# Flamingo-style gated block (cross attention and mixture of experts) on one core: merged constant loads, x by partition, and another order of the first steps

## What is computed

```python
ln_out = _ln(hidden_states, ln_w, ln_b)          # a layernorm of a layernorm
q  = _ln(_fp8_linear(ln_out, wq,  wq_scale,  q_in_scale))    # 16 heads of 128
k  = _ln(_fp8_linear(ln_out, wk,  wk_scale,  k_in_scale))    # 8 heads
v  =     _fp8_linear(ln_out, wv,  wv_scale,  v_in_scale)
qx = _ln(_fp8_linear(ln_out, wqx, wqx_scale, qx_in_scale))
kx, vx = split(ctx @ w_kv_x.T); kx = _ln(kx)
out = _fp8_linear(concat(attend(q, k, v), attend(qx, kx, vx)) / smooth, wproj, ...)
# _fp8_linear(x, w, ws, s) = (round_to_fp8(clip(x / s)) * s) @ w.T * ws
```

## Time and profile before

| | |
|---|---|
| median of 3 runs | 438.38 us (436.29 to 438.97) |
| profiled execution | 438.61 us |
| its span, first to last instruction | 436.8 us |
| mean granted TensorE clock | 0.969 |
| PE busy | 387.8 us (89%) |
| VectorE (DVE) busy | 352.9 us (81%) |
| ScalarE (ACT) busy | 294.6 us (67%) |
| GpSimd (POOL) busy | 278.0 us (64%) |

### The profile page before, as it was taken

The page is one execution under the profiler, slowest core; times in us unless marked ns, Lnnn a source line. Parts: engine busy times, 40 slices in busy tenths (PEclk is TensorE's granted clock), DMA queues, the critical chain, the costliest instruction groups (busy, mean ns, idle before and its releaser), DMA issues.

```text
span 436.8 us, 11224 instructions
## 1 busy us (share of the span) xinstructions
PE 387.8 (89%) x3626; PEld 288.6 (66%) x3626; DVE 352.9 (81%) x804; ACT 294.6 (67%) x621; POOL 278.0 (64%) x379
## 2 busy tenths in 40 slices
PE   0577799999999999999999999999998497999970
PEld 0445567667667767676766777676687286999960
DVE  5867979999999998999999999999889762334336
ACT  2598788777877777876877787787973315666510
POOL 2068866886787687688588677765574750366650
PEclk9999999999999999999999999999989688999995
DMA  8960868999980000000000000000194213444308
GB/s 209 261 228 2 106 90 259 253 287 286 243 230 3 0 0 0 0 0 0 0 0 0 0 0 0 0 2 2 33 434 194 96 67 98 124 132 136 99 22 277
DMA packets 34621, 45.57 MB, mean 104 GB/s; under 512 B 2970, under 2 KB 32031, under 8 KB 33696
## 3 DMA queue, kind: packets, MB, share of 16 engines
q1 hardware_dynamic: 26368, 35.34, 27.4%
q0 software_dynamic: 6944, 9.46, 9.9%
q10 hardware_dynamic: 1280, 0.41, 0.5%
HBM read 28.21 MB, written 24.19 MB: 120 GB/s over the span
## 4 chain that ended last, share of the span: by engine, by line
PE 73%; DVE 11%; ACT 4%; DMA 4%; issue 3%; POOL 3%; POOLq 0%; ACTq 0%; SPq 0%; DVEq 0%
PE proj_ps L972 18%; PE proj_ps L964 8%; PE score_ps L1001 8%; PE pv_ps L1024 8%; PE headT_ps L990 6%; PE out_ps L1034 6%; PE proj_ps L1138 4%; PE headT_ps L1138 3%; PE score_ps L990 3%; PE probT_ps L1010 3%; DMA cenf<-in_cen 2%; PE score_ps L1153 1%; DVE xs L1702 1%; DVE arena L1326 1%; PE pv_ps L1153 1%
## 5 line engine op out<-in xcount | busy, mean ns | idle before, releaser
L972 PE MATMUL proj_ps<-arena 128*128 128x512 f16 x384 | 100.0, 383 | 3.0 <-DVE arena L1356 3.0
L1364 DVE BATCH_NORM_STATS2 st<-rot 128x6 f32<-128x256 f32 x192 | 72.6, 419 | 10.6 <-ACT rot L710 10.0
L572 POOL TENSOR_TENSOR rot<-rot,cw 128x512 f32<-128x512 f32 x64 | 77.9, 1238 | 2.5
L710 ACT ACTIVATE rot<-proj_ps 128x512 f32<-128x512 f32 x96 | 56.1, 585 | 7.6 <-PE proj_ps L972 6.0
L972 PEld LDWEIGHTS proj_ps<-arena 128*128 (+1 forms) x384 | 32.5, 98 | 32.3 <-issue 3.8
L642 POOL DMA_INDIRECT ybuf<-arena,bslot x31 | 30.5, 984 | 31.3 <-DVE bslot L1612 14.6
L731 ACT ACTIVATE rot<-rot,cw 128x128 f32<-128x128 f32 x128 | 40.9, 391 | 11.0 <-POOL cw L566 10.4
L578 POOL TENSOR_TENSOR reg<-reg,rinv 128x512 f32<-128x512 f32 x32 | 33.4, 1044 | 21.9 <-DVE rinv L1374 21.9
L964 PE MATMUL proj_ps<-arena 128*128 128x512 f16 x192 | 46.7, 379 | 0.6 <-POOL arena L528 0.6
L1024 PEld LDWEIGHTS pv_ps<-reg,vv 64*128 64x128 f32 x512 | 31.1, 187 | 12.9 <-issue 9.7
L990 PE MATMUL headT_ps<-idf,rot 128*128 128x128 f32 x256 | 38.5, 273 | 0.1
(11 more groups left out here) (229 smaller groups left out, 850.2 us busy)
## 6 DMA issues: line engine op xcount, KB each, us to landing
zbuf<-fill SPq DMA_DIRECT2D x1, 16576.5 KB, 65.5
arena<-in_wffn SPq DMA_DIRECT2D x4, 1536.0 KB, 13.4
arena<-zbuf SPq DMA_DIRECT2D x30, 128.5 KB, 2.2
wkv_stage<-in_wkvN SPq DMA_DIRECT2D x1, 2048.0 KB, 15.4
wp_sb<-in_wpT POOLq DMA_DIRECT2D x1, 2048.0 KB, 16.4
wp_sb<-ybuf SPq DMA_DIRECT2D x8, 256.0 KB, 4.5
xs<-in_x SPq DMA_DIRECT2D x2, 512.0 KB, 5.5
vv<-in_wqN POOLq DMA_DIRECT2D x1, 1024.0 KB, 12.5
```

What stands on the lines that cost most here:

```text
L572: gp.tensor_tensor(r, r, cw[:, 4 * i:4 * i + 4].unsqueeze(2).to_broadcast([P, 4, D]), ALU.mult)\
L710: act.activation(raw[c % 2][i], proj_ps[i % 2][:, :], ACT.Copy).then_inc(proj_evac, 1)
L972: mm = pe.matmul(ps, lhs, w[kind][:, ch, 512 * b:512 * b + 512], start=(k == 0), stop=(k == 3))
L1364: ins = ve.bn_stats(st[:, 4 * i + h:4 * i + h + 2, :].rearrange("p h s -> p (h s)"), raw[c % 2][i][:, h * D:(h + 2) * D].rearrange("p (h d ...
```

## The change

The constants `colv`, `idf` and `cenf` become one array of 316 columns and one load; `rowv`, `trif` and `slots` become another of 186 columns. x is laid out by partition in HBM and loaded in three pieces: tile 0, tiles 1 to 3, tiles 4 to 7. VectorE takes the statistics of tile 0 first, has its root taken alone, and takes those of the other tiles around it; the other tiles are scaled by a second Newton step after tile 0's grid, and all of them are normalised there. PE transposes tile 0 before folds 0 and 1, then has both halves of the other transposes and folds 2 to 5 before step 0; ScalarE's list is changed to match.

```diff
+XG = [(0, 1), (1, NT // 2), (NT // 2, NT)]
+NCONST = NCOL + 2 * P
+NTABLE = NROWV + P + NT * TOPK
+EARLY = 6
@@ tiles
-        colv = sb("colv", [P, NCOL], F32)
...
+        consts = sb("consts", [P, NCONST], F32)
+        colv, idf, cenf = consts[:, 0:NCOL], consts[:, NCOL:NCOL + P], consts[:, NCOL + P:NCONST]
+        tables = sb("tables", [P, NTABLE], F32)
...
-            return range(4, NFOLD) if isinstance(n, int) and n == 0 else range(0)
+            return range(EARLY, NFOLD) if isinstance(n, int) and n == 0 else range(0)
@@ SP
-            for half in range(2):
-                sp.dma_start(xs[:, half * NHT * H:(half + 1) * NHT * H].rearrange("p (t d) -> p t d", t=NHT),
-                             x[half * NHT * P:(half + 1) * NHT * P, :].rearrange("(t p) d -> p t d", p=P))\
-                  .then_inc(ld_x[half], 16)
+            for i, (t0, t1) in enumerate(XG):
+                sp.dma_start(xs[:, t0 * H:t1 * H], x[:, t0 * H:t1 * H]).then_inc(ld_x[i], 16)
@@ ScalarE
-            act.dma_start(colv[:, :], cols).then_inc(ld_cols, 16)
-            act.dma_start(idf[:, :], ident).then_inc(ld_small, 16)
-            act.dma_start(cenf[:, :], cen).then_inc(ld_small, 16)
-            act.dma_start(rowv[:, :], rowc).then_inc(ld_route, 16)
-            act.dma_start(trif[:, :], tri).then_inc(ld_route, 16)
-            act.dma_start(slots[:, :], slot).then_inc(ld_route, 16)
+            act.dma_start(consts[:, :], cols).then_inc(ld_cols, 16)
+            act.preload_act_table(ACT.Tanh)
+            act.dma_start(tables[:, :], rowc).then_inc(ld_route, 16)
...
-            act.wait_ge(ld_small, 32)
...
-            root(0, tw[:, 0, :], tw[:, 1, :], tw[:, 2, :])
+            root(0, tw[:, 0, 0:1], tw[:, 1, 0:1], tw[:, 2, 0:1])
...
-            for j in range(2):
-                fold_high(j)
             act.wait_ge(xT0_done, 1)
             for c in range(HC):
                 act.activation(xT[:, c, 0:P], proj_ps[1][:, c * P:(c + 1) * P], ACT.Identity,
                                scale=col("lnw", c), bias=col("lnb", c)).then_inc(xT0_evac, 1)
+            for j in range(2):
+                fold_high(j)
+            root(1, tw[:, 0, 1:NT], tw[:, 1, 1:NT], tw[:, 2, 1:NT])
...
             inputs_out(0)
-            for j in range(2, 4):
+            inputs_out(1)
+            for j in range(2, EARLY):
                 fold_high(j)
...
-                if isinstance(n, int) and n == 0:
-                    inputs_out(1)
@@ PE
-            pe.wait_ge(ld_small, 32)
-            pe.wait_ge(cen_done, 1)
-            for j in range(2):
-                fold(j)
+            pe.wait_ge(ld_cols, 16)
             pe.wait_ge(xn_done, 1)
             for c in range(HC):
                 mm = pe.transpose(proj_ps[1][:, c * P:(c + 1) * P], xn[:, c * P:c * P + P], idf[:, :])
             mm.then_inc(xT0_done, 1)
+            pe.wait_ge(cen_done, 1)
+            for j in range(2):
+                fold(j)
...
             input_transposes(0)
+            input_transposes(1)
...
-                if isinstance(n, int) and n == 0:
-                    input_transposes(1)
...
-            for j in range(2, 4):
+            for j in range(2, EARLY):
                 fold(j)
@@ VectorE
+            row_stats(0, 1, ld_x[0])
+            inputs_variance(0, 1)
             ve.memset(oneh[:, :], 1.0)
             ve.memset(fill[:, 0:H], 0.0)
...
+            row_stats(1, NHT, ld_x[1])
+            inputs_scale(0, 0, 1)
...
             rows_normal(0, 1)
-            rows_normal(1, NHT)
+            row_stats(NHT, NT, ld_x[2])
+            inputs_variance(1, NT)
+            ve.wait_ge(tanh_done, 1)
+            ve.tensor_scalar(gate[:, 0:1], th[:, 0:1], col("s_proj"), None, ALU.mult)
+            link(ve.tensor_copy(gate[:, 1:2], th[:, 1:2]))
+            link(ve.tensor_scalar(gate[:, 2:3], gate[:, 0:1], col("s_pin"), None, ALU.mult))
...
-            for j in range(2):
-                fold_low(j)
-
...
                              .to_broadcast([P, 4, HC, P]), ALU.mult).then_inc(xin_done, 1)
+            for j in range(2):
+                fold_low(j)
             inputs_clip(0)
...
             ve.tensor_tensor(xq[:, 0:XW], ys[:, :], xm[:, :], ALU.subtract).then_inc(xgrid_done, 1)
+            inputs_scale(1, 1, NT)
+            rows_normal(1, NHT)
             rows_normal(NHT, NT)
-            for j in range(2, 4):
+            for j in range(2, EARLY):
                 fold_low(j)
```

52 lines of the change are left out of this document (23 added, 29 removed).

## The result

The changed kernel took 445.94 us (median of four runs, 443.42 to 446.70), the kernel before 437.71 us beside it (436.29 to 438.97): ratio 1.0179, interval 1.0126 to 1.0232. It is slower, by 8.2 us where 3.1 were forecast. The profiled execution took 446.70 us with a span of 444.9, that is 8.1 us over the span of before. The two ratios stand for 7.8 and 5.8 us, and their intervals together reach from 3.6 to 10.2.

The account below looks back on a forecast made before the run. The start's chain through VectorE, ScalarE and GpSimd was taken as the bound. First projection 6.2 us later, 3.0 given back by ScalarE, Ln 3.1 later: 438.61+3.1 = 441.7, less 0.23, so 441.5 us; range 438.0 to 446.0.

Parts of the forecast that it names:

- L, the constants: Start, ScalarE's queue: the merged constants land at 4.7 us, between 4.2 and 7.1, letting VectorE begin.
- Rival C: Start, ScalarE's queue: merged constants take two turns, landing at 7.1; VectorE's list moves 2.4 us, total 443.9; chance 0.12.
- Grid of tile 0: VectorE's list up to the first projection: 13.2 us from the constants, grid ready at 17.9, 1.5 us before the old 19.4.
- Grid to first projection: Second Newton, tiles 1 to 3, transposes and folds 2 to 5 hold the first projection to 25.7, 6.2 us later.
- First projection to its evacuation: PE's first projection: its result comes 1.9 us after its start, at 27.6, with 0.5 less as the other end.
- Evacuation to Ln: ScalarE's list: fold 6 follows after 0.5 us, then 8.44 us as before; Ln at 36.5, 3.1 us later.
- Ln to step 1's variance: GpSimd's unchanged list carries the Ln's shift to step 1's variance, about 13.3 us behind the Ln.
- rival B: x's last load waits behind wq, landing near 13; VectorE stands about 3 us, total 444.5; chance 0.17.
- phase of the later loop and measurement 1 us: Allowance of 1 us among this case's own unknowns, in the range 440 to 443.5.
- A: Tile 0's gain carries: first projection at the grid, before 22.5, with 3.0 us of ScalarE's list gone; 433.9 us; chance 0.06.
- D: Absorbed: a wait behind step 2 hides the late start, or the start is not bound as read; 438.4 us; chance 0.12.

Follow-up runs that it names:

- merged_only: Kernel before with only the merged constant and table loads and the Tanh table loaded early; x, orders and roots as before: ratio 1.0094, 443.2 us.
- hold_wq: Changed kernel with GpSimd issuing wq and what follows it only when x has landed: ratio 1.0113, 443.27 us.
- tables_late: Changed kernel with the loads of the tables and of the router issued behind tile 0's evacuation: ratio 1.0070, 448.77 us.
- x_two_loads: Changed kernel with x in the old two loads by rows, all else kept: ratio 1.0083, 443.63 us.
- folds_early_half_late: folds_early with the second half of the transposes and its evacuations moved behind step 0's Ln and Exp: ratio 0.9986, 443.7 us.
- second_half_late: project_first with the second half of the transposes and its evacuations moved behind step 0's Ln and Exp: ratio 1.0013, 440.29 us.
- project_first_no_hold: project_first without the wait ahead of wq: ratio 1.0047, 448.06 us.
- start_later: Kernel before with only three scratch fills on VectorE ahead of the first normalising, as a pure delay: ratio 1.0100, 444.43 us.
- after_again: The changed kernel, unchanged, measured again on another chip: ratio 1.0133, 445.5 us.
- transposes_back: Changed kernel with the second half of the transposes and folds 4 and 5 put back behind the first projection: ratio 1.0093, 443.63 us.
- folds_early: Kernel before with only folds 4 and 5 moved ahead of step 0: ratio 0.9896, 444.62 us.
- project_first: hold_wq with the first projection ahead of both halves of the transposes, normalised x in the output weights' tile: ratio 1.0109, 443.92 us.

## Why the prediction was right and wrong

**The direction was right, and for the reason given.** The first projection waits behind both halves of the transposes, and these behind VectorE's list; ScalarE gives part back; GpSimd's list carries the rest to step 1's variance. Step by step, forecast and measured:

- *L, the constants*: 4.7 forecast, 3.95 measured (and 3.82 to 4.89 over the other kernels with the merge). The five times larger load cost nothing over `colv`. Rival C (two turns, 7.1) did not happen.
- *Grid of tile 0*: 17.9 forecast, 20.17 measured. This is the step that failed. VectorE waited 3.19 us; the better L gives 0.75 back; the rest of the list is right to 0.2 us (17.9-0.75+3.19 = 20.34).
- *Grid to first projection* (second Newton, tiles 1 to 3, transposes, folds 2 to 5): 7.8 forecast, 28.04-20.17 = 7.87 measured. The hidden work is indeed on the path.
- *First projection to its evacuation*: 1.9 forecast, 1.50 measured; the four matmuls took 1.31 us, between the 1.86 and the 1.03 of the earlier trace rows.
- *Evacuation to Ln*: 0.5+8.44 = 8.9 forecast, 8.79 measured.
- *Ln to step 1's variance*: 13.4 forecast, 13.37 measured.

So the start cost 4.93 us instead of 3.1 (5.4 to 5.8, an estimate, against a `cenf` as in the other kernels), and the mis-sized term is one: the landing of x's last load, which I put at about 9 and which came at 12.4, and between 10.2 and 11.7 in the other kernels with x in three loads. It was rival B, with a chance of 0.17, a landing "near 13" and 444.5 us. Its sum holds at the Ln: 3.1+3.19-0.75, less 0.6 for the small differences above, is 4.9. In the total it does not.

Why B was underrated can be said with numbers. I held against it that SP's second load had landed before POOL's first, and concluded on the order of turns from one profile. `merged_only` shows that this order was not given: with nothing but ScalarE's loads changed, that same second load went from 6.8 to 9.8 us. I had costed the merge at the constants' own queue, and its price stands on another queue. The 3.0 us stand against at most 128 KB more ahead of x, 0.5 us at the 235 GB/s of the earlier trace rows, so it is not the bytes. The prediction took from the Trainium skill (DMA: Bandwidth & Descriptors, Queues, rings and completion order) that each DMA engine goes round the queues that have work, a packet of descriptors at a time; by that a longer request of ScalarE's would take turns that x would have had. The trace agrees in the sign, and the rule gives no size. That a whole load is one turn, whatever its length, was my own reading of the landing order. It priced the longer load at nothing for the other queues, and that is what failed. `hold_wq` gives 0.6 to 2.2 us to wq, and `tables_late` clears the tables. x in two loads landed at 10.2 and 11.1 (`x_two_loads`, `merged_only`), in three and with wq not held at 10.9 to 12.4, so the third load costs between nothing and 2.2 us. Why 8.5 us instead of 6.2 to 7.0 remain with wq held back is open.

**The total.** 3.1 us of the 8.1 arose behind attention. I had "phase of the later loop and measurement 1 us" for this; the profiles show 91.9 to 101.0 us for that part. The measured 445.94 lies just inside the stated 438.0 to 446.0, and beyond the 440 to 443.5 of the case's own unknowns; that it is still inside is luck, since two things that the sum did not have, 1.8 us of a late x and 3.1 us behind attention, happened to add up to no more. Against the 3.1 being the change's doing speak these: the pure delay cost 2.9 to 5.9 us, so a late start as such does not slow it; the part's length does not follow the start (`folds_early_half_late` has the earliest start and the longest end); and 1.2 of the 3.1 are the sixteen matmuls at half clock, which were as slow in `second_half_late`. For it speaks that the changed kernel's profile of 95.7 us has no late step in the experts' loop and is still the longest of those without one; only one profile was taken of before, so this is not settled. `merged_only` and `hold_wq` were measured a little above what their start accounts for (from 2.5 for 2.0, from 3.4 for 2.7); the late `cenf` in the profile of before, 0.5 to 0.9 us, can be the difference. How much of the first 8.2 is chance can't be told closer than that, with 5 us of it, or somewhat more, accounted for at the start.

**The other rivals.** A asked for a first projection before 22.5. `project_first_no_hold` had that, 19.48, and was not faster than before: the deciding point was badly chosen, since the transposes hold ScalarE wherever the projection stands. Its argument against A (tiles 1 to 7 are 3.3 us behind the grid) was the right one. D was false: `start_later` shows no slack.

**What each part is worth**, at the Ln. The merged constants, with the early Tanh table: +2.0 us. The order can be told from the landing of x by counting from the statistics of tiles 4 to 7 to the Ln: 24.26 us in `merged_only` with the old order, 25.9 in after, `after_again`, `x_two_loads` and `hold_wq` with the new one. So the new order costs 1.6 us. The rest of the 4.9 is when x lands, 0.9 us sooner in `x_two_loads` than in `merged_only` and 0.5 to 1.3 later in the changed kernel. Within the order, the transposes' second half and two folds ahead of the projection are +1.0 (`transposes_back`), and the second half taken out of the stretch altogether -2.4 (`second_half_late`).

No kernel here was shown to be faster than before by more than its measurement tells. The best start is `folds_early_half_late`'s, 2.25 us earlier, of which 0.9 are `cenf`'s landing.

## What to carry to other kernels

Moving work into an engine's idle time helps only if the work's inputs are there in that time: look at which engine's list makes them. Here PE and ScalarE were idle, but the transposes hung on VectorE, the engine that had made them idle. Work is best moved past the point that the next stage waits for (here the Ln), not up to it.

A load that is made larger or earlier can be paid on the other queues: read every early load's landing, and ask who needs the one that will be late. An order of landings read from one profile is not a rule, and a rival that hangs on it deserves more than 0.17.

Where an end part varies by several us between kernels that have the same instructions there (here 91.9 to 101.0 us), judge a change of the start by its own stage (here the variance of step 1) and use a run with a pure delay to see what passes through.

## What the runs showed of the hardware that was not expected

**VectorE held by GpSimd.** In `folds_early` VectorE normalised four tiles in 2.58 us, which take 1.38 otherwise; in its timeline

```profile
17.97 0.69 DVE L1356 TENSOR_TENSOR arena<-ys,xm 128x1024 f16<-128x1024 f16 x1
18.57 2.58 DVE L1313 TENSOR_SCALAR rot<-xs,tw,tn 128x256 f32<-128x256 f32 x4
```

(and so in `folds_early_half_late`, 2.58 again), and in GpSimd's at that time

```profile
18.09 1.04 POOL L516 CAST arena<-reg 128x512 f16<-128x512 f32 x1 [14.43 <-ACT reg L686]
19.21 1.15 POOL L518 TENSOR_TENSOR arena<-reg,arena 128x512 f16<-128x512 f32 x1
```

In `project_first_no_hold` it is seen instruction by instruction, VectorE

```profile
19.25 0.61 DVE L1260 TENSOR_TENSOR tw<-tw 128x7 f32<-128x7 f32 x1
19.89 0.17 DVE L1261 TENSOR_TENSOR tw<-tw 128x7 f32<-128x7 f32 x1
20.09 1.01 DVE L1262 TENSOR_SCALAR tw<-tw 128x7 f32<-128x7 f32 x1
```

against GpSimd

```profile
19.23 0.61 POOL L515 CAST arena<-reg 128x512 f16<-128x512 f32 x1 [15.57 <-ACT reg L681]
19.92 1.15 POOL L517 TENSOR_TENSOR arena<-reg,arena 128x512 f16<-128x512 f32 x1
```

Two operations on 7 columns, 0.16 and 0.17 us in after (at 20.09 and 20.49), end at 19.86 and 21.10, just when GpSimd's end (19.84 and 21.07); the one between, which falls into GpSimd's gap, takes 0.17. The Trainium skill (SBUF — State Buffer, Who interferes with whom) describes a port pair of the two engines that one instruction holds for its whole length; the trace agrees. A fold's high half that is moved forward can so cost VectorE 1.2 us in the middle of the critical list. In `folds_early` PE then stood 1.39 us idle for this normalising, and ScalarE waited 1.90 us for the second half of the transposes where it had waited 0.26 before; that took back most of what the two folds (1.1) and the short first projection (0.8) had freed, and 0.3 were left.

A slow second projection stands in that stretch too, at the lower level of the clock (windows, columns as before), but it took nothing:

```profile
20.00:24.60 4.60, 3.39 (x24) 3.33 (x25) 3.80 (x8) 2.62 (x5) 0.36 (x1) 0.50 1.04 290
24.60:26.60 2.00, 2.00 (x8) 0.56 (x7) 1.50 (x2) 1.71 (x3) 1.30 (x2) 0.50 0.98 398
```

ScalarE waited 0.32 us for it, yet from fold 6's high half to the Ln it took 8.47 us, before 8.44.

**Four matmuls, two durations.** The second projection of `folds_early` took 1.91 us in a stretch at 0.50 (1.2 GHz), its first 1.02 at 1.00; PE had been idle for 2.05 us ahead of the first and for 1.39 us ahead of the transposes between the two. Before, the first projection took 1.86 although the granted clock reads 1.00 for it. At a reading of 1.00 it took anything between 1.02 and 1.91 us in the other kernels: 1.91 in `project_first`, 1.87 in `start_later`, 1.80 in `second_half_late`, 1.31 in after, but 1.03 in `after_again` and `hold_wq`. In `merged_only` alone the column reads lower over it, 0.61, and it took 1.57. So the column alone doesn't tell a matmul's speed here; its own duration does.

**What one queue's landing depends on.** x's second half of 512 KB, issued at 1.3 us (in three loads 1.7), landed 6.2 to 7.0 us later with the old constant loads, 9.0 to 10.7 with the merged ones and 8.5 to 8.6 with these and wq held back. The same kernel's two profiles differ by 0.8 us (10.7 and 9.9), which moves its start by 0.8 us as well.
